# Eight sequences of modulated attention and a spiking feed-forward: a fourth feature tile, keys' rows by parts, sooner transfers

## What is computed

```python
mod = (silu(c) @ wmod).reshape(8, 6, 1, 128)       # sa, ca, ga, sb, cb, gb
h = layernorm(x) * (1 + ca) + sa
q, k, v = split(h @ qkv_w.T + qkv_b)               # 16 heads of 8
q, k = rope(q), rope(k)
attn = softmax(causal(q @ k.T / sqrt(8)))
x = x + ga * ((attn @ v) @ proj_w.T + proj_b)
h = layernorm(x) * (1 + cb) + sb
y = square(relu(h @ W_fc.T)) @ W_proj.T
x = x + gb * spikes(y) / 5                          # 5 steps of a threshold neuron, written as 5 comparisons
```

## Time and profile before

| | us |
|---|---|
| median of 3 runs | 444.27 |
| lowest, highest run | 440.36, 444.5 |
| profiled execution, its own time | 443.15 |
| its span (first to last instruction) | 441.4 |
| lies around the span | 1.75 |

### The profile page before, as it was taken

One profiled execution on the slowest core, in us unless ns is written; L12 is line 12 of the kernel. 1 busy time (PEld: TensorE's weight loads), 2 busy tenths in 40 slices (PEclk: granted clock), 3 DMA queues, 4 the chain that ended last, 5 costly groups with the idle time before them and its releaser, 6 DMA issues.

```text
span 441.4 us, 15622 instructions
## 1 busy us (share of the span) xinstructions
PE 390.9 (89%) x6599; PEld 253.1 (57%) x6599; DVE 329.3 (75%) x730; ACT 256.8 (58%) x447; POOL 126.1 (29%) x163
## 2 busy tenths in 40 slices
PE   2778899888999989998899999998998889988885
PEld 2327555555656755666457654765566646753653
DVE  6659995886886988878986997699866777541176
ACT  8203465565676756765666665766665457566523
POOL 6714310430343043503342234304330220040020
PEclk9989999999999999999999999999999899998999
DMA  7056363243314233242415251323233050011001
GB/s 214 22 161 169 99 218 88 70 116 102 104 45 119 75 101 93 80 122 49 137 50 139 64 138 48 117 72 99 67 113 86 16 146 6 25 45 27 3 1 49
DMA packets 26050, 38.53 MB, mean 87 GB/s; under 512 B 5796, under 2 KB 20716, under 8 KB 23692
## 3 DMA queue, kind: packets, MB, share of 16 engines
q1 hardware_dynamic: 25980, 37.53, 29.8%
HBM read 26.35 MB, written 8.65 MB: 79 GB/s over the span
## 4 chain that ended last, share of the span: by engine, by line
PE 41%; DMA 18%; DVE 13%; ACT 10%; POOL 6%; issue 5%; SPq 5%; ACTq 0%; POOLq 0%; DVEq 0%
PE o_bank L611 10%; DMA kf<-k_scr 9%; PE d_bank L528 7%; DVE negmax L978 6%; PE t_bank L593 6%; PE s_bank L548 5%; DMA rden<-r_scr 4%; ACT probs L827 4%; PE a_bank L528 3%; DMA r_scr<-rden_c 2%; POOL parts L1303 2%; PE s_bank L528 2%; SPq L440 2%; PE t_bank L528 2%; POOL o_n L1325 2%
## 5 line engine op out<-in xcount | busy, mean ns | idle before, releaser
L978 DVE TENSOR_REDUCE negmax<-s_bank 128x1 f32<-128x512 f32 (+7 forms) x368 | 192.9, 566 | 56.9 <-PE s_bank L554 54.6
L827 ACT ACTIVATE probs<-t_bank 128x512 f32<-128x512 f32 x288 | 163.0, 594 | 89.8 <-PE t_bank L598 84.5
L548 PE MATMUL s_bank<-kf,qf 126*64 126x512 bf16 (+7 forms) x1024 | 118.7, 293 | 11.8 <-DMA kf<-k_scr 6.2
L593 PE MATMUL t_bank<-qf,kf 128*64 128x512 bf16 (+7 forms) x1024 | 113.3, 290 | 10.8 <-ACT probs L827 9.8
L611 PE MATMUL o_bank<-probs,v 128*32 128x512 f32 (+7 forms) x1024 | 75.1, 412 | 0.0
L548 PEld LDWEIGHTS s_bank<-kf,qf 126*64 126x64 bf16 x1024 | 50.6, 111 | 40.6 <-DVE negmax L978 19.9
L554 PE MATMUL s_bank<-causal,identb 128*64 128x64 bf16 x1024 | 72.6, 195 | 0.0
L598 PE MATMUL t_bank<-causal_t,identb 128*64 128x64 bf16 x1024 | 64.8, 195 | 0.0
L593 PEld LDWEIGHTS t_bank<-qf,kf 128*64 128x64 bf16 x1024 | 41.4, 110 | 35.1 <-ACT probs L827 14.4
L598 PEld LDWEIGHTS t_bank<-causal_t,identb 128*64 128x64 bf16 x1024 | 48.1, 111 | 9.3 <-issue 0.2
L554 PEld LDWEIGHTS s_bank<-causal,identb 128*64 128x64 bf16 x1024 | 47.1, 112 | 8.3 <-issue 8.1
(11 more groups left out here) (145 smaller groups left out, 455.9 us busy)
## 6 DMA issues: line engine op xcount, KB each, us to landing
qf<-q_scr SPq DMA_DIRECT2D x15, 576.0 KB
kf<-k_scr SPq DMA_DIRECT2D x45, 192.0 KB
q_scr<-parts SPq DMA_DIRECT2D x24, 128.0 KB, 1.7
k_scr<-parts SPq DMA_DIRECT2D x24, 128.0 KB, 1.7
xa<-in_x SPq DMA_DIRECT2D x8, 256.0 KB, 3.9
o_t<-o_raw SPq DMA_DIRECT2D x60, 32.0 KB, 2.4
rden<-r_scr SPq DMA_DIRECT2D x15, 128.0 KB
out_y<-count SPq DMA_DIRECT2D x7, 256.0 KB, 6.7
```

What stands on the lines that cost most here:

```text
L548: nc.tensor.matmul(bank[C * a:C * (a + 1), col:col + keys], qf[0:KS, slot, 2 * p + a, C * i:C * (i + 1)], kf[0:KS, slot, 2 * p + a, 0:keys ...
L593: nc.tensor.matmul(bank[C * a:C * (a + 1), col:col + w], kf[0:KX, slot, 2 * p + a, C * kb:C * (kb + 1)], qf[0:KX, slot, 2 * p + a, C * kb: ...
L827: nc.scalar.activation(probs[:, v, :], t_bank[u % 2][:, :], ACT.Exp, scale=SCALE).then_inc(e_done, 1)
L978: last = nc.vector.tensor_reduce(own[:, i, p:p + len(same)], cols, AX.X, ALU.max, negate=True)
```

## The change

The rings get a fourth tile; its rows are cleared by ScalarE in the start. The row of a feature becomes 24j + 8i + d. The queries' DMA leads with a broadcast over 3, then the 24 rows. Each of the keys' three DMAs now takes one part j and leads with a broadcast over 3, then the 8 features; it can be issued once its own part is stored. For half 2b+4 the queries and the first two parts of the keys are issued at the end of iteration b, the third part in iteration b+1, behind its store. The projection moves from slot 16 to 17 with its residual (18 to 19), the second half's reciprocals from 10 to 9. Four tiles share memory with others: `sq` with `relu`, `rest` with `rot_s`, `wmod_sb` with `relu`, `ones_row` with `count`; the second and third step of `rotary` therefore wait for `split_done` in place of `whole_done`.

```diff
-RING = 3
+RING = 4
-D_AT = {16: PROJ, 25: T2, 27: FC, 29: FC + 1, 31: FC + 2, 33: FC + 3}
+D_AT = {17: PROJ, 25: T2, 27: FC, 29: FC + 1, 31: FC + 2, 33: FC + 3}
...
-        rest = sb("rest", [P, 2, SEQ])
+        rest = rot_s
...
-        sq = sb("sq", [P, NF, SEQ])
+        sq = relu
+        wmod_sb = relu[:, 0:2, :].rearrange("p i c -> p (i c)")[:, 0:6 * P]
...
+        ones_row = count[0:MR, 0, 0:SEQ // 2].bitcast(BF16)
...
                 sp.dma_start(qf[0:FR, n % RING, own],
-                             q_rows.unsqueeze(1).to_broadcast([NPART * HD, NPART, many, SEQ])).then_inc(done, 16)
+                             q_rows.unsqueeze(0).to_broadcast([NPART, NPART * HD, many, SEQ])).then_inc(done, 16)
-            def spread_keys(n, own=slice(0, HH), done=None):
+            def spread_keys(n, own=slice(0, HH), done=None, some=None):
...
-                sp.wait_ge(k_stored, 16 * Q_STORES * (b + 1))
-                k_rows = k_scr[b % 2].rearrange("j (d h) c -> d j h c", h=H)[:, :, heads]
                 m = HD * NPART
-                for i in range(NPART):
-                    sp.dma_start(kf[m * i:m * (i + 1), n % RING, own], k_rows).then_inc(done, 16)
+                first, last = (0, NPART) if some is None else some
+                sp.wait_ge(k_stored, 16 * (Q_STORES * b + (2 if last < NPART else Q_STORES)))
+                for j in range(first, last):
+                    k_rows = k_scr[b % 2, j].rearrange("(d h) c -> d h c", h=H)[:, heads]
+                    sp.dma_start(kf[m * j:m * (j + 1), n % RING, own],
+                                 k_rows.unsqueeze(0).to_broadcast([NPART, HD, many, SEQ])).then_inc(done, 16)
...
                 if 0 < b < final:
                     store_part(b + 1, 1, 2)
-                if 0 < b < final:
-                    spread(2 * b + 2)
+                    spread_keys(2 * b + 2, some=(2, NPART))
...
                 if b + 2 < NB:
                     store_part(b + 2, 1, 1)
+                    spread_queries(2 * b + 4)
+                    spread_keys(2 * b + 4, some=(0, 2))
...
             place_values(0)
+            clear(3, qf)
+            clear(3, kf)
             modulate1(1)
...
-                reach(dve, whole_done, 2 * (b - 1) + qk + 1)
+                reach(dve, whole_done if step == 0 else split_done, 2 * (b - 1) + qk + 1)
...
-                    if at == (8 if b == final else 10):
+                    if at == (8 if b == final else 9):
                         reciprocals(b - 1, 1)
-                    if at == 18:
+                    if at == (18 if b == final else 19):
                         residual1(b - 1)
```

More of the change, by code:

```diff
@@ L181, in adaln_kernel @@
         ct_sb = sb("ct_sb", [P, NB])
-        wmod_sb = sb("wmod_sb", [P, 6 * P])
         cos_sb = sb("cos_sb", [P, SEQ])
@@ L188, in adaln_kernel @@
         causal_t = sb("causal_t", [P, P], BF16)
-        ones_row = sb("ones_row", [MR, SEQ], BF16)
         minus_half = sb("minus_half", [P, NT])
@@ L409, in spread_queries @@
                 sp.dma_start(qf[0:FR, n % RING, own],
-                             q_rows.unsqueeze(1).to_broadcast([NPART * HD, NPART, many, SEQ])).then_inc(done, 16)
-            def spread_keys(n, own=slice(0, HH), done=None):
+                             q_rows.unsqueeze(0).to_broadcast([NPART, NPART * HD, many, SEQ])).then_inc(done, 16)
+            def spread_keys(n, own=slice(0, HH), done=None, some=None):
                 b, half = divmod(n, 2)
                 heads = slice(HH * half + own.start, HH * half + own.stop)
+                many = own.stop - own.start
                 done = done or feat[n % RING]
-                sp.wait_ge(k_stored, 16 * Q_STORES * (b + 1))
-                k_rows = k_scr[b % 2].rearrange("j (d h) c -> d j h c", h=H)[:, :, heads]
                 m = HD * NPART
-                for i in range(NPART):
-                    sp.dma_start(kf[m * i:m * (i + 1), n % RING, own], k_rows).then_inc(done, 16)
+                first, last = (0, NPART) if some is None else some
[4 more added lines that the diff above has]
+                                 k_rows.unsqueeze(0).to_broadcast([NPART, HD, many, SEQ])).then_inc(done, 16)
             def spread(n, *some):
@@ L466, in _ @@
             sp.wait_ge(ones_made, 1)
-            sp.wait_ge(zeros_made[2], 2)
+            for slot in (2, 3):
+                sp.wait_ge(zeros_made[slot], 2)
             sp.dma_start(kf[KS:KX].rearrange("r s h c -> r (s h) c"),
```

## The result

The changed kernel takes 586.4 us (median of 4 runs, 585.43 to 588.63) against 443.42 before: ratio 1.325, interval 1.317 to 1.333. It was forecast slower, at 645 us; the range was 500 to 730.

What follows compares the result with a forecast made beforehand. Before, TensorE was taken to bound the kernel, busy 89% of the span; the new patterns were to leave features on three engines. 443.15 + 157 for six batches + 45 for the start = 645 us, range 500 to 730.

Steps and rivals of the forecast that it cites:

- The mechanism: Feature copies: the leading dimension deals out engines, so both new patterns run on three, 21.1 us for a half.
- the packet time: Feature copies: one packet of 8 KB holds one engine for 0.44 us, counted while the old keys move.
- Both bounds: Limits on a packet's time on one engine: 0.29 us gives 530 us in all, 0.50 us gives 691.
- The start: Features of halves 0 to 3 in a row, 84.4 us plus gaps: some 45 us more with the cold clock.
- T0: In each batch, the moment when SyncE has issued the second part of the keys; 279.5 in the trace before.
- The steady batch by its steps: One batch from T0 to the next T0, in five steps: 70.5 us, 23.0 more than the 47.5 before.
- the clock: TensorE restarts slow after a stall: 1.6 us lost each, two stalls a batch, 3.2 us.
- The clears: Two new clears of 1.89 us each fall into ScalarE's 7.11 us wait before `modulate1` and cost nothing.
- The store behind the bulk: Third part's store queues behind queries and keys, holding SyncE; with unchanged rates, up to 1 us a batch, hidden.
- The slots: Projection, residual and reciprocals a slot on or back: save 5.7 us at best, cost 1.3 us a batch at worst; drowned.
- the faster rival (435 us): Leading 3 does not deal out the work, rates stay; sooner issue and later projection end TensorE's waits: 435 us, chance 0.07.
- the one at 443: Rates stay; the third part's store behind 960 KB costs up to 1 us a batch against equal savings: 443 us, chance 0.06.

Runs made afterwards that it cites:

- e1: The kernel before with only the two new copy patterns, queries and keys led by a broadcast over 3: 584.2 us, ratio 1.319.
- e3: The kernel before with only the keys' DMAs led by a broadcast over 3, queries as before: 505.4 us, ratio 1.141.
- e2: The changed kernel with the two old copy patterns, the keys' three DMAs together in iteration b+1: 445.5 us, ratio 1.008.
- e4: The changed kernel in its whole order, rows renumbered so queries lead with 24 rows and keys with 8 features, repeats inside: 441.5 us, ratio 1.001.
- e5: The kernel before with k_scr stored by feature, so that each keys' DMA leads with 24 rows: 445.3 us, ratio 1.011.
- e9: The changed kernel with the old patterns and the even half's whole spread back in iteration b+1: 433.2 us, ratio 0.984.
- e10: As e9 (changed kernel, even half's whole spread back in iteration b+1), but with e4's patterns: 432.1 us, ratio 0.983.
- e6: The kernel of e2 with e5's keys, led by 24 rows: 444.2 us, ratio 1.010.
- e7: The changed kernel with e5's patterns and the even half's whole spread back in iteration b+1: 437.0 us, ratio 0.994.

## Why the prediction was right, and where it was off

**The mechanism** was right and is shown: e1 has the whole loss from the two patterns; e3 keeps the queries wide and has 65 of the 144 us; e2 and e4 keep everything else and have none. The Trainium skill (DMA: Bandwidth & Descriptors, "Why a DMA increments its semaphore by 16 and not by 1") gives 3, 8 and 12 engines for leading 3, 8 and 24; the trace agrees: the shares while features move are 0.19, 0.46 and 0.81 of 16: 3.1, 7.4 and 13.0. The last includes other traffic.

**The term that was mis-sized** is the packet time. I took 0.44 us, counted where eight engines ran. With three it is 0.31 (after, e3), with eight 0.33 or 0.44 by what they read, with twelve 0.58 (e5). So it is no constant of an engine, and the figure of the old pattern did not hold for the new one. That it falls because fewer engines run is not shown, since the pattern changed with their number.

Both bounds were misread, too. The lower one divides 455 GB/s by 16, but that row has a share of 1.08: 455 / (16 x 1.08) is 26.3 GB/s, 0.31 us and not 0.29. Read so, the copy of `rows`, led by a broadcast as the new patterns are, had the packet time that was measured. The upper one takes 8 GB/s off for small packets, but 34 packets of 8 KB in 2 us are the 139 GB/s by themselves, and 14 under 512 B can hold at most 4; by eight engines that is 0.47 us and not 0.50. Likewise the 13.9 engines for the queries come from a single stretch of 1 us, and the 1.08 shows that such a short one can overcount; over 282 to 284 us, the start of the copy included, the share is 0.70, 11 engines.

**Where the 59 us between 645 and 586 lie.** The start was to cost 45 us, and the first T0 came 34 later than before (126.4 for 92.1). The six batches and the end were to cost 157 and cost 109, as a batch grew by 65.2 - 47.5 = 17.7 us and not by 26.2. The 96 packets of a batch, 0.13 us too long each, make 12.5 us, more than those 8.5: with the right packet time and all else as it was, the forecast would have come out too low. What else in these steps was longer than forecast no run takes apart.

**The steady batch by its steps.** To the third keys' DMA: 20 forecast, 271.19 - 255.14 = 16.1 measured. From there to the reciprocal: 7; 6.9. To the odd half's queries: 7.0; 286.87 - 278.12 = 8.8. To its landing: 22.8; 18.0. To the next T0: 13.7; 15.2. The sum was 70.5 plus 3.2 for the clock, and is 64.9. The first and the fourth step, made of packets, are 8.7 us shorter; the third and the fifth, which follow a restart, are 3.3 longer: that is where the clock's price stands, forecast at 3.2. By row, the clock is 0.50 in 278 to 280 and 0.51 in 306 to 308, at the lower of its two levels, after 9.65 and 6.45 us without a matmul. TensorE's busy time rose by 29.0 us in the whole run for the same matmuls; I had 6 x 3.2 = 19 and a share of the start.

**The clears** fell into ScalarE's gap as forecast:

```profile
29.01 0.78 ACT L856 ACTIVATE hT<-a_bank,mod 128x512 f32<-128x512 f32 x1 [3.32 <-PE a_bank L635]
```

`modulate1` starts at 29.01, where it was 29.09, and the gap before it is 3.32 us where it was 7.11: two clears of 1.89 less.

**The store behind the bulk** was seen in the prediction, priced in the narrow version (it held SyncE until 271.19), and called up to 1 us a batch and hidden in the wide one. That was too little: the sooner issue, which puts the store there, costs 12.3, 9.4 and 7.2 us in the three pairs (e2 and e9, e4 and e10, e6 and e7; the first two ran on different chips, and by the ratios it is 2.4, 1.8 and 1.6%). That is 1.2 to 2.1 us for each of the six batches. The Trainium skill (DMA: Bandwidth & Descriptors, "Queues, rings and completion order") says that an engine takes descriptors in ring order; the trace agrees, with 13.23 us for a store that lands in 1.75 when nothing is ahead.

**The slots** were called drowned here and worth 5.7 us at best. Alone they are worth some 5 us in both runs, while the waits on `o_n` fell by only 2.6 and 3.3. In the two traces TensorE's busy time is also lower, 386.5 and 385.6 us for 390.9, and SyncE waits 9.3 us for the ring in both, for 22.9 before. What of this makes the rest of the gain is open.

**Of the signs named ahead**, the share of 0.19, the reciprocals' wait on `den` (66.8 us in 7 waits), SyncE's wait for the stores and the clock came as said; 50 to 60 GB/s was 82, 25 us of waits a batch were 16 to 18, and TensorE is busy 72%, not 60. The waits for `den` and for the stores do not mark the loss, though, as e1 has it without them. Were the rates to stay, as the faster rival (435 us) and the one at 443 supposed, the change would be no gain: e2 and e4 keep wide patterns and take 445.5 and 441.5. That is the second of these rivals, and for its reason, the store behind the bulk.

## What to carry to other kernels

Before a copy pattern is rewritten, look at the leading dimension on both sides: it decides how many engines carry the copy, and a broadcast over a few copies put first narrows it to that few. What is stored and then waited for goes out ahead of any large transfer on the same queue, not behind it, even if the large one could start sooner. Take the price of a packet from a copy of the same form as the new one, and not from the one that it replaces. And keep edits that ride along apart: here a 1% gain from three moved slots was buried under a 32% loss.

## What was not expected of the hardware

- **The packet time hangs on what is read as well as on the engines in use.** It is 0.31 us with three engines (after), 0.44 with eight (before), 0.58 with twelve or thirteen (e5): 82, 139 and 184 GB/s. But it is 0.31 also with all sixteen in the copy of `rows`, which reads one row for every partition, and with eight it went to 0.33 when each row was read three times in a row in place of three different ones (e4). The queries at 283 us, led by 24 and read so as well, take 0.87 x 16 / 34 = 0.41. Whether the 0.44 of the old keys comes from the distance between their rows in HBM (128 KB between parts) or from reading no row again at once stays open; in e5 the 24 rows lay one behind the other and were the slowest. No packet of 8 KB takes less than 0.307 us in the traces before and after; 0.31 or less take 87% of them after and 13% before. So the three engines ran near their best, and there were too few of them.
- **SyncE's own issues last longer at times with the narrow patterns.** Four copies to `den` are issued in 2.71 us at 272.67 and in 5.56 at 293.41, right behind a spread and a store of the output. In the start, with three spreads queued, single issues took longer still:

```profile
37.68 7.36 SPq L392 DMA_DIRECT2D xa<-in_x  x1
45.09 9.27 SPq L482 DMA_DIRECT2D g_scr<-gate_t  x1
```

In the kernel before, with three spreads queued as well, these issues are

```profile
34.53 0.57 SPq L388 DMA_DIRECT2D xa<-in_x  x1
35.15 0.47 SPq L472 DMA_DIRECT2D g_scr<-gate_t  x1
```

e1 has such issues at the same place (4.92 and 9.52 us), e10 with wide patterns has not (0.45 and 0.69). The profile shows the time inside the issue, and no wait. What length of queue sets it off was not tried.
